# Choice of experts moved from VectorE to GpSimd, and a narrower wait at the seam between projections and attention

## The chip, the cores and the metric

One core of one Trainium2 chip runs the whole program in one launch. The metric is device time in microseconds. TensorE is PE in the tables (PEld is its weight load), VectorE is DVE, ScalarE is ACT, GpSimd is POOL, and SyncE is SP, which here only issues transfers.

## The reference, cut to what matters

The input `x` has 8 batches of 1024 tokens of 256 numbers. Two branches start from the normalised `xn`:

```
xn = layernorm(x)
s  = attention(layernorm(xn) * scale + bias) + xn      # 16 heads of 64, low-rank q/k/v, rotary, softmax
logits = xn @ router_w.T                               # 8 experts
k_probs, k_idx = top_k(softmax(logits), 2)             # normalised over the two
rank = position of this (token, choice) among all that chose the same expert
keep = rank < capacity
out_buf = silu(xn @ w1[e]) @ w2[e]                     # for each expert's kept rows
combined = sum over the two of k_probs * out_buf[e, rank] * keep
out = x + s * silu(combined + xn)
```

"The choice of experts" in this document is the arithmetic behind the two largest logits: each choice's rank in its expert's list, the row of a table in which its token is entered (`fill`), its factor in the sum (`mix`), and for each group of 256 table rows the expert whose weights it takes (`widx`).

## The kernel before, in words

The program has four stages, one behind the other on each engine: projections (`project_parts`, eight batches of 1024 tokens), attention (`attend_parts`, 64 pairs of heads), experts (`expert_parts`, 71 groups of rows), and the combination. Every engine has its own instruction list, written out by hand; there is no planner. Engines wait for each other on semaphores, and each works its list strictly in order. What changes is the seam between projections and attention, and the first pair of heads.

Projections end with the last batch's compressed vectors `cpt`. SP stores them to memory (L203) and ACT holds the wait `stored` before its first copy of attention (L1178, `pj["stored"](e)` in the prologue of `scalar`). Tiles are laid over each other: `at_rawq` and `at_rawk`, into which ACT copies the first projected queries and keys (L1130), lie over the tile from which the rows `xn` are stored; `rt_tot` and its neighbours lie over the tile from which `cpt` is stored. `stored` waits for both kinds of store.

The prologue of attention then prepares the first pair. ACT copies queries and keys out of PSUM (L1130); SP makes copies with neighbouring rows exchanged (L828, `at_swpq`, `at_swpk`); DVE turns them (L942 by the cosines, L946 the exchanged rows by the sines, L950 the sum) and makes `at_kdif` and `at_step` (L959, L966, L967); PE meanwhile computes the last batch's value vectors (L540), which ACT copies out and SP stores (L207). A loop of six steps k = 0..5 finds row maxima of the first pair: PE L1299 and L1302, then ACT L1147 (`gain`) and DVE L974 (`maximum`), for two heads in turn. In it ACT also writes and sends the negated maxima (`negate` L1162, `max_rows` L1168, two transfers that ACT itself issues), and behind it PE and ACT project and copy the third pair's queries (L1338, L1130).

`body` is one pair: eight steps g = 0..7, in each of which PE has two score tiles (L1279), two tiles of maxima, and the value products of the step before (L1292); ACT has two exponentials (L1124), two `gain`s, and copies; DVE has two maxima, running sums of the exponentials (L985) and the turning of the pair after the next. From the second pair on PE also has two sets of denominators (L1346), which ACT copies out (`den_copy` L1157). The next pair's first maxima come out of this pair's steps, so that an engine that is late by more than a step stops the others.

The choice of experts (`route_parts`) is woven into this. PE makes two products of the one-hot tiles, column totals (L621) and prefix sums (L624), into `at_st`. DVE does the rest in slices of a generator, `next(choice)`: copy of the totals (L642), running sum (L644), small sizes (L652 to L657), ranks (L661, L664) in the prologue; four products (L668, L669), four sums over the experts (L673, L675), rows (L678 to L683), factors (L686 to L690) and `widx` (L692 to L695) in the body of the first pair. PE waits with `ranked` for the ranks before its first body, ACT and POOL with `done` for everything: ACT at step g = 5 of the first pair, before `out_copy` writes `mid_osb`, which lies over the one-hot tiles and `rt_rank`; `mid_den`, first written at step g = 0 of the second pair, lies over `rt_tmp`. POOL then enters tokens in the table, pair by pair (L911 to L916). The table is first read before the last pair.

Of the kernel before, what the change touches and what calls it, by code (L numbers as in the profile page):

```python
# [99 lines left out]
def project_parts(nc, ctx, io, scr, keep):  # L100


    with ExitStack() as tiles:
# [127 lines left out]
        def stored(e):  # L231
            for s in s_xs:
                e.wait_ge(s, 16 * (NBATCH // 2 + 1))
            for s in s_cs:
                e.wait_ge(s, 32 * (NBATCH // 2 + 1))
# [267 lines left out]
        def tensor(e):  # L503
# [73 lines left out]
            with e.Fori(0, NBATCH // 2 - 1) as it:  # L577
# [6 lines left out]
                "stored": stored, "values_stored": values_stored, "chosen": chosen, "emptied": emptied}  # L584


def route_parts(nc, ctx, keep, pj):

    with ExitStack() as tiles:
# [13 lines left out]
        tmp = [by_expert(sb(f"tmp{k}", [P, C])[:, :]) for k in range(4)]  # L603
        tot, cum = sb("tot", [P, NE, NT]), sb("cum", [P, NE, NT])
        dif, p2, den = (sb(n, [P, NT]) for n in ("dif", "p2", "den"))
        rk, pos, over, kept, row, blk_of = (sb(n, [P, NT, 2])[:, :, :] for n in ("rk", "pos", "over", "kept", "row", "blk_of"))
        need, end, base = (sb(n, [P, NE]) for n in ("need", "end", "base"))
        past, who = sb("past", [P, GROUPS, NE - 1]), sb("who", [P, GROUPS])
        s_v, s_mm, s_dif, s_exp, s_mul, s_done = (sem(n) for n in ("v", "mm", "dif", "exp", "mul", "done"))
        sides = [slice(n * C // 2, (n + 1) * C // 2) for n in range(2)]  # L610

        def scalar(e):
            e.wait_ge(s_dif, 1)
            e.activation(p2[:, :], dif[:, :], ACT.Exp).then_inc(s_exp, 1)

# [11 lines left out]
        def vector(e, pt, pp):  # L627
# [12 lines left out]
            e.wait_ge(s_mm, 2)  # L640
            pj["stored"](e)
            then(e.tensor_copy(tot[:, :, :], pt.rearrange("p (t e) -> p e t", e=NE)))  # L642
            yield
            then(e.tensor_tensor_scan(flat(cum), newe[:, :], flat(tot), 0.0, ALU.mult, ALU.add))  # L644
# [6 lines left out]
            yield  # L651
            e.tensor_tensor(out=dif[:, :], in0=m[1][:, :], in1=m[0][:, :], op=ALU.subtract).then_inc(s_dif, 1)  # L652
# [3 lines left out]
            then(e.tensor_tensor_scan(end[:, :], ones[:, 0:NE], need[:, :], 0.0, ALU.mult, ALU.add))  # L656
# [3 lines left out]
            yield  # L660
            then(e.tensor_tensor(out=cum[:, :, :], in0=cum[:, :, :], in1=tot[:, :, :], op=ALU.subtract))  # L661
            yield
            e.wait_ge(s_mm, 4)
            then(e.tensor_tensor(out=rank, in0=by_expert(pp), in1=cum[:, :, :].rearrange("p e t -> p t e"), op=ALU.add))  # L664
            e.sem_inc(s_done, 1)
            for k in range(2):
                yield
                e.tensor_tensor(out=tmp[k], in0=oh[k], in1=rank, op=ALU.mult).then_inc(s_mul, 1)  # L668
                e.tensor_tensor(out=tmp[2 + k], in0=oh[k], in1=base3, op=ALU.mult).then_inc(s_mul, 1)  # L669
            for k in range(2):  # L670
                yield
                e.wait_ge(s_mul, 2 * k + 1)
                e.tensor_reduce(out=rk[:, :, k], in_=tmp[k], axis=AX.X, op=ALU.add).then_inc(s_mul, 1)  # L673
                e.wait_ge(s_mul, 2 * k + 2)
                e.tensor_reduce(out=pos[:, :, k], in_=tmp[2 + k], axis=AX.X, op=ALU.add).then_inc(s_mul, 1)  # L675
            yield
            e.wait_ge(s_mul, 8)
# [3 lines left out]
            then(e.scalar_tensor_tensor(out=row, in0=row, scalar=float(NSLOT // P), in1=blk_of, op0=ALU.mult, op1=ALU.add))  # L681
            then(e.tensor_scalar(over, rk, float(CAP), FAR, ALU.is_ge, ALU.mult))
            e.tensor_tensor(out=keep["fill"][:, :, :], in0=row, in1=over, op=ALU.add).then_inc(s_done, 1)  # L683
            yield
# [6 lines left out]
            yield  # L691
            then(e.tensor_tensor(out=past[:, :, :], in0=grp[:, :].unsqueeze(2).broadcast_to((P, GROUPS, NE - 1)),  # L692
                                 in1=end[:, 0:NE - 1].unsqueeze(1).broadcast_to((P, GROUPS, NE - 1)), op=ALU.is_ge))
            then(e.tensor_reduce(out=who[:, :], in_=past[:, :, :], axis=AX.X, op=ALU.add))
            e.tensor_scalar(keep["widx"][:, :], who[:, :], float(P), part[:, 0:1], ALU.mult, ALU.add).then_inc(s_done, 1)  # L695

        def ranked(e):
            e.wait_ge(s_done, 1)
# [4 lines left out]
        return {"vector": vector, "scalar": scalar, "tensor": tensor, "ranked": ranked, "done": done}  # L703


def attend_parts(nc, ctx, below, bridge, io, scr, keep, pj, rt):


    with ExitStack() as tiles:
# [195 lines left out]
        def gpsimd(e):  # L905
            def body(i, *_):
                if isinstance(i.n(), int) and i.n() == 0:
                    pj["blanked"](e)
                    rt["done"](e)
# [9 lines left out]
            def prologue():  # L919
                e.memset(zeros[:, :], 0.0).then_inc(s_blank, 1)  # L920
                e.wait_ge(s_blank, 1)

# [10 lines left out]
        def vector(e, ex_vector):  # L933
# [74 lines left out]
            choice = rt["vector"](e, *route_at)  # L1008

            def prologue():  # L1010
# [16 lines left out]
                for k in range(6):  # L1027
# [6 lines left out]
                    if k in (3, 5):  # L1034
                        next(choice)
# [7 lines left out]
                    if k >= 3:  # L1043
                        next(choice)
# [4 lines left out]
            def body(i, prev, ahead):  # L1049
# [3 lines left out]
                for g in range(NG):  # L1053
# [38 lines left out]
                    if not prev and g < 4:  # L1092
                        next(choice, None)
                        next(choice, None)
                    if not prev and g == 4:
                        for _ in choice:
                            pass
                        e.memset(ones[:, :], 1.0)
# [19 lines left out]
        def scalar(e, pj_value, ex_scalar):  # L1118
# [52 lines left out]
            def prologue():  # L1171
# [6 lines left out]
                pj["stored"](e)  # L1178
# [12 lines left out]
                for k in range(6):  # L1191
# [1002 lines left out]
```

## Time and profile before

| | us |
|---|---|
| runs of the kernel before, median of 3 | 3825.41 (3824.31 to 3827.25) |
| profiled execution, its own time | 3827.14 |
| its span from first to last instruction | 3825.6 |
| PE busy | 3727.7 (97%) |
| DVE busy | 3382.1 (88%) |
| ACT busy | 2811.3 (73%) |
| POOL busy | 861.9 (23%) |

Busy shares are averages over the four stages. Times in the rows below count from the first instruction of the profiled execution; projections end at about 210 us, and the first pair's body begins on PE at 264.04 us.

### The profile page before, as it was taken

What the parts mean: (1) busy time and instruction counts of PE and PEld (TensorE: products, weight loads), DVE (VectorE), ACT (ScalarE), POOL (GpSimd) and SP (SyncE); (2) the same over time, 40 slices, a digit from 0 to 9 for tenths busy, and PEclk for the clock granted to TensorE, in tenths of its full rate; (3) what the DMA queues carried; (4) which work ended last, traced back from release to release, by engine and by line L of the source; (5) the groups of instructions that cost most, each with busy time, mean ns of one, the idle gap of its engine ahead of it and who ended that gap; (6) DMA issues with size and microseconds to landing.
All of it is one profiled execution on the core that took longest, in us unless ns stands there. A gap on an engine that the chain in (4) does not pass through costs nothing. (4 is left out here: it accounts for less than half of the span.)

```text
span 3825.6 us, 77720 instructions
## 1 busy us (share of the span) xinstructions
PE 3727.7 (97%) x24340; PEld 2379.8 (62%) x24340; DVE 3382.1 (88%) x4656; ACT 2811.3 (73%) x4075; POOL 861.9 (23%) x796
## 2 busy tenths in 40 slices
PE   7969999999999999999999999999999999999999
PEld 5744444444444444444444444444499999999899
DVE  8869999999999999999999999999777777777699
ACT  5757887878787878787787878787766666666565
POOL 2205544510000000000000000000166666666400
PEclk9989999999999999999999999999999999999999
DMA  7964554544444444434444444443366666666697
GB/s 262 355 226 148 153 166 150 169 134 137 126 137 126 136 126 126 136 112 140 118 139 121 137 126 137 126 134 105 115 217 218 219 217 219 220 217 220 203 367 261
DMA packets 397301, 659.74 MB, mean 172 GB/s; under 512 B 140142, under 2 KB 288751, under 8 KB 361137
## 3 DMA queue, kind: packets, MB, share of 16 engines
q1 hardware_dynamic: 349984, 449.85, 37.8%
q0 software_dynamic: 45200, 208.52, 15.8%
q8 instruction: 35, 0.57, 0.1%
q10 hardware_dynamic: 2048, 0.53, 0.1%
q14 instruction: 34, 0.27, 0.0%
HBM read 453.07 MB, written 138.81 MB: 155 GB/s over the span
## 5 line engine op out<-in xcount | busy, mean ns | idle before, releaser
L1124 ACT ACTIVATE at_ex<-at_st 128x1024 f32<-128x1024 f32 x1024 | 1047.1, 1023 | 121.8 <-PE at_st L1279 98.8
L1292 PE MATMUL at_pv<-at_ex,at_v 128*64 128x512 f32 x4096 | 992.6, 605 | 0.0
L1147 ACT ACTIVATE at_fr<-at_fr 128x512 f32<-128x512 f32 x1024 | 599.9, 586 | 343.7 <-PE at_fr L1302 291.0
L974 DVE TENSOR_REDUCE at_mx<-at_fr 128x1 f32<-128x512 f32 x1024 | 703.7, 687 | 126.1 <-PE at_fr L1299 73.1
L985 DVE TENSOR_TENSOR at_sum<-at_sum,at_ex 128x1024 f32<-128x1024 f32 x512 | 624.9, 1221 | 12.7 <-ACT at_ex L1124 1.8
L1572 POOL DMA_INDIRECT seam_stage<-in_w,keep_widx x142 | 139.2, 980 | 1960.4 <-DVE at_rotk L950 1886.9
L1292 PEld LDWEIGHTS at_pv<-at_ex,at_v 128*64 128x64 f32 x4096 | 248.7, 136 | 509.6 <-issue 494.2
L1302 PE MATMUL at_fr<-at_kfar,at_qh 64*128 64x512 f32 x1024 | 466.4, 455 | 19.0 <-DVE at_mx L974 11.0
L1299 PE MATMUL at_fr<-at_kdif,at_qh 64*128 64x512 f32 x1024 | 471.5, 460 | 4.6 <-DVE at_mx L974 2.4
L1299 PEld LDWEIGHTS at_fr<-at_kdif,at_qh 64*128 64x128 f32 x1024 | 188.2, 184 | 418.9 <-issue 411.5
L1756 PE MATMUL ex_h<-ex_xT,ex_w 128*128 128x256 f32 x3408 | 423.4, 284 | 4.2 <-issue 4.2
L1772 PE MATMUL ex_o<-ex_w,ex_hT 128*128 128x256 f32 x3408 | 425.2, 284 | 0.9 <-DVE ex_out L1653 0.9
L1756 PEld LDWEIGHTS ex_h<-ex_xT,ex_w 128*128 128x128 f32 x3408 | 416.7, 193 | 6.0 <-issue 6.0
L1772 PEld LDWEIGHTS ex_o<-ex_w,ex_hT 128*128 128x128 f32 x3408 | 412.4, 191 | 1.1 <-DVE ex_out L1653 1.1
L1279 PE MATMUL at_st<-at_qh,at_kh 64*128 64x512 f32 x2048 | 405.8, 392 | 3.3 <-DMA at_top<-at_mneg 3.1
L1279 PE MATMUL at_st<-at_ql,at_kh 64*128 64x512 f32 x2048 | 403.8, 389 | 0.0
L1279 PE MATMUL at_st<-at_qh,at_kl 64*128 64x512 f32 x2048 | 403.5, 389 | 0.0
L1692 ACT ACTIVATE ex_w<-seam_stage 128x1024 fp32r<-128x1024 f32 x142 | 142.6, 1051 | 286.5 <-PE ex_o L1772 282.3
L985 DVE TENSOR_TENSOR at_sum<-at_ex 128x1024 f32<-128x1024 f32 x256 | 311.2, 1216 | 2.8 <-ACT at_ex L1124 2.8
L1578 POOL DMA_INDIRECT scr_eo<-ex_out,mid_slots x142 | 253.3, 1784 | 221.8 <-DVE ex_out L1653 168.2
L1302 PEld LDWEIGHTS at_fr<-at_kfar,at_qh 64*128 64x128 f32 x1024 | 188.2, 184 | 93.6 <-issue 76.3
L1279 PEld LDWEIGHTS at_st<-at_qh,at_kl 64*128 64x128 f32 x2048 | 193.7, 184 | 44.6
(183 smaller groups left out, 5657.1 us busy)
## 6 DMA issues: line engine op xcount, KB each, us to landing
at_cq<-scr_c SPq DMA_DIRECT2D x62, 1024.0 KB
at_ck<-scr_c SPq DMA_DIRECT2D x62, 1024.0 KB
scr_v<-pj_v SPq DMA_DIRECT2D x64, 512.0 KB, 6.7
at_swpq<-at_rawq SPq DMA_DIRECT2D x128, 256.0 KB
at_swpk<-at_rawk SPq DMA_DIRECT2D x128, 256.0 KB
at_v<-scr_v SPq DMA_DIRECT2D x64, 512.0 KB
mid_rec<-scr_rec SPq DMA_DIRECT2D x256, 128.0 KB
scr_o<-mid_oT SPq DMA_DIRECT2D x64, 512.0 KB
```

Source lines behind the costliest of these rows:

```text
L974: e.reduce_max(mx[k // QB][:, h * QB + k % QB:h * QB + k % QB + 1], fr[h][:, :], AX.X).then_inc(s_tr[h], 1)
L985: e.tensor_tensor(out=acc, in0=ex[k - 1][:, :, :] if first else acc, in1=ex[k][:, :, :], op=ALU.add).then_inc(s_sum, 1)
L1124: e.activation(ex[k][:, :, :], st[u % 2][:, :, :], ACT.Exp, scale=SCALE).then_inc(s_exp, 1)
L1147: e.activation(fr[h][:, :], fr[h][:, :], ACT.Relu).then_inc(s_pos[h], 1)
L1279: mm = e.matmul(st[u % 2][:, h, :], kk[rows[h], :] if t == 3 else kk[rows[h], keys], qq[rows[h], bank[n]], start=(t == 0 and kt < 2), stop ...
L1292: mm = e.matmul(pv[n][rows[h], :], v[i.u][:, kt, rows[h]], ex[kt][:, h, :], start=(kt == 0), stop=(kt == KT - 1))
L1299: return e.matmul(fr[h][:, :], query_tile(j, k, h), kdif[j.u][rows[h], :], start=True, stop=True)
L1302: return e.matmul(fr[h][:, :], query_tile(j, k, h), kfar[j.u][rows[h], :], start=False, stop=True, skip_group_check=True)
L1578: e.indirect_dma_start(out=scr["eo"], out_offset=bass.IndirectOffsetOnAxis(ap=slots[:, g * GT + c:g * GT + c + 1], axis=0), in_=out[g % 2] ...
L1692: e.activation(w2_half(a.u, 0, k), half2(raw2[a.u], k), ACT.Copy).then_inc(s_w2h, 1)
L1756: mm = e.matmul(phid[:, j, f % 2 * GP:(f % 2 + 1) * GP], w1[q][:, ws, f, k, :], xT[q][:, xs, k, :], start=(ws + xs + k == 0), stop=(ws == ...
L1772: mm = e.matmul(po[:, c, 0:D], hT[q][:, hh, f, c * P:(c + 1) * P], w2[q][:, ws, f, :], start=(hh + ws + f == 0), stop=(hh == 1 and f == NF ...
```

## The change

There are four edits.

1. ACT's first wait of attention becomes `rows_stored`, which waits for the stores of the rows `xn` only. The wait for the stores of `cpt` stays in front of the copy of the totals.
2. ACT takes both products out of PSUM (`take_total` at k = 2, `take_prefix` at k = 3). DVE keeps one instruction of the choice, the running sum over 512 columns, now at k = 5.
3. Everything else of the choice is written again for POOL, as one list of 50 instructions behind the sum, each waiting for the one before. Sums over the experts become three additions of halves, a scan of eight becomes a copy and seven additions, the reciprocal becomes a power of -1, the comparison of groups with ends becomes seven compares and four additions, and a fused operation becomes two.
4. PE waits for the two copies instead of the ranks; DVE (g = 4) and ACT (g = 5) of the first pair wait for POOL's products (`spread`); ACT waits for all of the choice (`done`) at g = 0 of the second pair; ACT's exponential of the choice moves from g = 1 to g = 2. At the end of the prologue ACT sends the negated maxima behind `gain(first, 4, 1)` and not ahead of it, and the first half of the third pair's queries is projected at k = 4 and copied at k = 5.

```diff
+        def rows_stored(e):
+            for s in s_xs:
+                e.wait_ge(s, 16 * (NBATCH // 2 + 1))
         def stored(e):
-            for s in s_xs:
-                e.wait_ge(s, 16 * (NBATCH // 2 + 1))
+            rows_stored(e)
...
+        def vector(e):
+            e.wait_ge(s_taken, 1)
+            e.tensor_tensor_scan(cum[...], newe[:, :], tot[...], 0.0, ALU.mult, ALU.add).then_inc(s_scan, 1)
+        def take_total(e, pt):
+            e.wait_ge(s_mm, 2)
+            pj["stored"](e)
+            e.activation(tot[:, :, :], pt.rearrange("p (t e) -> p e t", e=NE), ACT.Copy).then_inc(s_taken, 1)
+        def take_prefix(e, pp):
+            e.wait_ge(s_mm, 4)
+            e.activation(rank, by_expert(pp), ACT.Copy).then_inc(s_taken, 1)
...
+        def gpsimd(e):
+            e.wait_ge(s_taken, 1)
+            e.tensor_tensor(out=dif[:, :], in0=m[1][:, :], in1=m[0][:, :], op=ALU.subtract).then_inc(s_dif, 1)
+            e.wait_ge(s_scan, 1)
...
-            then(e.tensor_tensor_scan(end[:, :], ones[:, 0:NE], need[:, :], 0.0, ALU.mult, ALU.add))
+            then(e.tensor_copy(end[:, 0:1], need[:, 0:1]))
+            for k in range(1, NE):
+                then(e.tensor_tensor(out=end[:, k:k + 1], in0=end[:, k - 1:k], in1=need[:, k:k + 1], op=ALU.add))
...
+            for k in range(2):
+                then(e.tensor_tensor(out=by_expert(tmp[:, k, :]), in0=oh[k], in1=rank, op=ALU.mult))
+                then(e.tensor_tensor(out=by_expert(tmp[:, 2 + k, :]), in0=oh[k], in1=base3, op=ALU.mult))
             e.sem_inc(s_done, 1)
-            for k in range(2):
-                e.tensor_reduce(out=rk[:, :, k], in_=tmp[k], axis=AX.X, op=ALU.add).then_inc(s_mul, 1)
-                e.tensor_reduce(out=pos[:, :, k], in_=tmp[2 + k], axis=AX.X, op=ALU.add).then_inc(s_mul, 1)
+            for n in (NE // 2, NE // 4, NE // 8):
+                then(e.tensor_tensor(out=each[:, :, 0:n], in0=each[:, :, 0:n], in1=each[:, :, n:2 * n], op=ALU.add))
...
-            then(e.reciprocal(keep["mix"][:, :, 0], den[:, :]))
+            then(e.tensor_scalar(dif[:, :], ones[:, 0:NT], -1.0, None, ALU.mult))
+            then(e.tensor_tensor(out=keep["mix"][:, :, 0], in0=den[:, :], in1=dif[:, :], op=ALU.pow))
...
-            then(e.tensor_tensor(out=past[:, :, :], in0=grp..., in1=end..., op=ALU.is_ge))
-            then(e.tensor_reduce(out=who[:, :], in_=past[:, :, :], axis=AX.X, op=ALU.add))
+            for k in range(NE - 1):
+                then(e.tensor_scalar(past[:, :, k], grp[:, :], end[:, k:k + 1], None, ALU.is_ge))
+            then(e.tensor_tensor(out=past[:, :, 0:3], in0=past[:, :, 0:3], in1=past[:, :, 3:6], op=ALU.add))
+            then(e.tensor_tensor(out=past[:, :, 0:1], in0=past[:, :, 0:1], in1=past[:, :, 6:7], op=ALU.add))
+            then(e.tensor_tensor(out=past[:, :, 0:1], in0=past[:, :, 0:1], in1=past[:, :, 1:2], op=ALU.add))
+            then(e.tensor_tensor(out=who[:, :], in0=past[:, :, 0], in1=past[:, :, 2], op=ALU.add))
+            then(e.tensor_scalar(who[:, :], who[:, :], float(P), part[:, 0:1], ALU.mult, ALU.add))
+            e.tensor_copy(keep["widx"][:, :], who[:, :]).then_inc(s_done, 1)
...
         def ranked(e):
+            e.wait_ge(s_taken, 2)
+        def spread(e):
             e.wait_ge(s_done, 1)
...
@@ attention, ACT
-                pj["stored"](e)
+                pj["rows_stored"](e)
...
+                    if k == 2:
+                        rt["take_total"](e, route_at[0])
+                    if k == 3:
+                        rt["take_prefix"](e, route_at[1])
                     if k == 4:
                         negate(first, 0)
-                        e.wait_ge(s_init, 2)
-                        max_rows(first, 0)
+                    if k == 5:
+                        proj_copy(third, Q, 0, pv[1])
                     gain(first, k, 1, s_y)
+                    if k == 4:
+                        e.wait_ge(s_init, 2)
+                        max_rows(first, 0)
-                for n in range(NH2):
-                    proj_copy(third, Q, n, pv[1])
+                proj_copy(third, Q, 1, pv[1])
...
                     if g == 5 and not prev:
+                        rt["spread"](e)
+                    if g == 0 and isinstance(i.n(), int) and i.n() == 1:
                         rt["done"](e)
@@ attention, PE
-                e.wait_ge(s_raw[K], 4)
-                project(third, Q, 0, pv[1])
+                    if k == 4:
+                        e.wait_ge(s_raw[K], 4)
+                        project(third, Q, 0, pv[1])
```

## Rows read from the trace of the kernel before

**Rows 1.** The page: busy time of the engines, their shares of the span.
```profile
PE 3727.7 (97%) x24340; PEld 2379.8 (62%) x24340; DVE 3382.1 (88%) x4656; ACT 2811.3 (73%) x4075; POOL 861.9 (23%) x796
```

**Rows 2.** Timeline of ACT at the seam: start, length, line, [idle before].
```profile
207.43 1.03 ACT L445 ACTIVATE pj_c<-pj_pa 128x1024 f32<-128x1024 f32 x1 [0.86 <-PE pj_pa L554]
224.39 1.09 ACT L1130 ACTIVATE at_rawq<-at_pv 128x512 f32<-128x512 f32 x2 [15.94 <-DMA scr_c<-pj_cpt]
```

**Rows 3.** Timeline of SP's queue at the seam.
```profile
207.91 2.94 SPq L203 DMA_DIRECT2D scr_c<-pj_cpt  x2
225.50 1.19 SPq L828 DMA_DIRECT2D at_swpq<-at_rawq  x2
```

**Rows 4.** Windows: us, busy PE, PEld, DVE, ACT, POOL; PEclk, DMA share, GB/s.
```profile
211.00:214.00 3.00, 0.00 (x0) 0.00 (x0) 0.00 (x0) 0.00 (x0) 0.00 (x0) 0.71 1.04 419
...
220.00:223.00 3.00, 0.00 (x0) 0.00 (x0) 0.00 (x0) 0.00 (x0) 0.00 (x0) 0.50 0.84 352
...
229.00:232.00 3.00, 3.00 (x14) 2.42 (x13) 2.97 (x3) 1.48 (x2) 0.00 (x0) 0.94 0.53 210
...
264.04:301.94 37.90, 30.20 (x161) 15.45 (x162) 35.42 (x55) 23.88 (x35) 6.62 (x10) 0.92 0.38 119
```

**Rows 5.** Timeline of DVE, prologue and first body.
```profile
228.52 1.22 DVE L946 TENSOR_TENSOR at_swpq<-at_swpq,at_sin 128x1024 f32<-128x1024 f32 x1 [1.10 <-DMA at_swpq<-at_rawq]
...
260.85 1.03 DVE L664 TENSOR_TENSOR rt_rank<-at_st,rt_cum 128x512 f32<-128x512 f32 x1
...
265.83 0.68 DVE L974 TENSOR_REDUCE at_mx<-at_fr 128x1 f32<-128x512 f32 x1
```

**Rows 6.** Timeline of PE, from the prologue to the second body.
```profile
238.18 0.50 PE L1299 MATMUL at_fr<-at_kdif,at_qh 64*128 64x512 f32 x1
...
267.54 0.38 PE L1299 MATMUL at_fr<-at_kdif,at_qh 64*128 64x512 f32 x1
...
310.53 0.50 PE L1299 MATMUL at_fr<-at_kdif,at_qh 64*128 64x512 f32 x1
...
312.71 0.39 PE L1299 MATMUL at_fr<-at_kdif,at_qh 64*128 64x512 f32 x1
```

**Rows 7.** Timeline of ACT at the end of the prologue; ACTq is its transfers' issue.
```profile
255.02 1.81 ACTq L1168 DMA_DIRECT2D at_top<-at_mneg  x2
256.87 0.58 ACT L1147 ACTIVATE at_fr<-at_fr 128x512 f32<-128x512 f32 x1 [1.94 <-issue]
```

**Rows 8.** Waits in 262 to 311 us: total, times, longest.
```profile
PE at_fr L1302 <- DVE at_mx L974: 6.9, 4, 3.6
```

**Rows 9.** Timeline of PE: denominators in the middle of the second and third body.
```profile
332.53 1.07 PE L1346 MATMUL at_pv<-at_sum,mid_ones 128*32 128x512 f32 x8
372.14 1.07 PE L1346 MATMUL at_pv<-at_sum,mid_ones 128*32 128x512 f32 x8
```

**Rows 10.** Timeline of POOL, small and powering instructions and a fill.
```profile
1.04 0.21 POOL L269 MEMSET early_zero<- 128x142 int32 x1
...
16.24 0.29 POOL L275 TENSOR_SCALAR pj_veps<-pj_mv 128x4 f32<-128x4 f32 x1 [1.70 <-DVE pj_mv L331]
16.61 1.05 POOL L277 TENSOR_TENSOR pj_rstd<-pj_veps,pj_minus_half 128x4 f32<-128x4 f32 x1
...
184.95 2.21 POOL L259 TENSOR_TENSOR pj_rstd<-pj_veps,pj_minus_half 128x8 f32<-128x8 f32 x1 [0.18 <-POOL pj_veps L257]
187.12 0.52 POOL L920 MEMSET at_zeros<- 128x512 f32 x1
...
318.71 1.25 POOL L911 COPY at_fill_i<-keep_fill 128x2 int32 x1 [4.03 <-DMA scr_table<-at_tok_i,at_fill_i]
```

**Rows 11.** Line L259: ns min/median/max of one, first and last start.
```profile
L259 POOL TENSOR_TENSOR pj_rstd<-pj_veps,pj_minus_half x14: 1665/1686/2570, 24.5 to 185.0; 128x8 f32<-128x8 f32 x14
```

**Rows 12.** Timeline of DVE beside POOL's instruction at 184.95.
```profile
185.67 1.23 DVE L395 TENSOR_TENSOR pj_cpt<-pj_c,pj_cpt 128x1024 fp32r<-128x1024 f32 x1
```

**Rows 13.** POOL's groups by line: busy us, mean ns of one, idle before.
```profile
L911 POOL COPY at_fill_i<-keep_fill 128x2 int32 x56 | 34.8, 621 | 182.1 <-DMA scr_table<-at_tok_i,at_fill_i 182.1
L912 POOL COPY at_tok_i<-keep_tok 128x2 int32 x56 | 15.0, 269 | 0.0
```

More of the change, by code:

```diff
@@ L602, in route_parts @@
         oh = [by_expert(early[f"oh{k}"][:, :]) for k in range(2)]
-        tmp = [by_expert(sb(f"tmp{k}", [P, C])[:, :]) for k in range(4)]
+        tmp = sb("tmp", [P, 4, C])
         tot, cum = sb("tot", [P, NE, NT]), sb("cum", [P, NE, NT])
         dif, p2, den = (sb(n, [P, NT]) for n in ("dif", "p2", "den"))
-        rk, pos, over, kept, row, blk_of = (sb(n, [P, NT, 2])[:, :, :] for n in ("rk", "pos", "over", "kept", "row", "blk_of"))
+        over, kept, row, blk_of = (sb(n, [P, NT, 2])[:, :, :] for n in ("over", "kept", "row", "blk_of"))
         need, end, base = (sb(n, [P, NE]) for n in ("need", "end", "base"))
         past, who = sb("past", [P, GROUPS, NE - 1]), sb("who", [P, GROUPS])
-        s_v, s_mm, s_dif, s_exp, s_mul, s_done = (sem(n) for n in ("v", "mm", "dif", "exp", "mul", "done"))
+        s_v, s_mm, s_dif, s_exp, s_taken, s_scan, s_done = (sem(n) for n in ("v", "mm", "dif", "exp", "taken", "scan", "done"))
         sides = [slice(n * C // 2, (n + 1) * C // 2) for n in range(2)]
@@ L670, in vector @@
-            for k in range(2):
-                yield
-                e.wait_ge(s_mul, 2 * k + 1)
-                e.tensor_reduce(out=rk[:, :, k], in_=tmp[k], axis=AX.X, op=ALU.add).then_inc(s_mul, 1)
-                e.wait_ge(s_mul, 2 * k + 2)
-                e.tensor_reduce(out=pos[:, :, k], in_=tmp[2 + k], axis=AX.X, op=ALU.add).then_inc(s_mul, 1)
-            yield
-            e.wait_ge(s_mul, 8)
+            e.wait_ge(s_taken, 2)
+            then(e.tensor_tensor(out=rank, in0=rank, in1=cum[:, :, :].rearrange("p e t -> p t e"), op=ALU.add))
@@ L678, in vector @@
+            sums = each[:, :, 0].rearrange("p (k t) -> p t k", k=4)
+            rk, pos = sums[:, :, 0:2], sums[:, :, 2:4]
             then(e.tensor_tensor(out=row, in0=rk, in1=pos, op=ALU.add))
@@ L680, in vector @@
             then(e.tensor_scalar(blk_of, blk_of, -WHOLE, float(1 - NSLOT), ALU.add, ALU.mult))
-            then(e.scalar_tensor_tensor(out=row, in0=row, scalar=float(NSLOT // P), in1=blk_of, op0=ALU.mult, op1=ALU.add))
+            then(e.tensor_scalar(row, row, float(NSLOT // P), None, ALU.mult))
+            then(e.tensor_tensor(out=row, in0=row, in1=blk_of, op=ALU.add))
             then(e.tensor_scalar(over, rk, float(CAP), FAR, ALU.is_ge, ALU.mult))
-            e.tensor_tensor(out=keep["fill"][:, :, :], in0=row, in1=over, op=ALU.add).then_inc(s_done, 1)
-            yield
+            then(e.tensor_tensor(out=row, in0=row, in1=over, op=ALU.add))
+            e.tensor_copy(keep["fill"][:, :, :], row).then_inc(s_done, 1)
             e.wait_ge(s_exp, 1)
@@ L687, in vector @@
             then(e.tensor_scalar(den[:, :], p2[:, :], 1.0, None, ALU.add))
[L688 removed]
+            then(e.tensor_scalar(dif[:, :], ones[:, 0:NT], -1.0, None, ALU.mult))
+            then(e.tensor_tensor(out=keep["mix"][:, :, 0], in0=den[:, :], in1=dif[:, :], op=ALU.pow))
             then(e.tensor_tensor(out=keep["mix"][:, :, 1], in0=p2[:, :], in1=keep["mix"][:, :, 0], op=ALU.mult))
             e.tensor_tensor(out=keep["mix"][:, :, 0:2], in0=keep["mix"][:, :, 0:2], in1=kept, op=ALU.mult)
[L691 to L695 removed]
+            for k in range(NE - 1):
[6 more added lines that the diff above has]
+            e.tensor_copy(keep["widx"][:, :], who[:, :]).then_inc(s_done, 1)
         def ranked(e):
+            e.wait_ge(s_taken, 2)
+        def spread(e):
             e.wait_ge(s_done, 1)
@@ L701, in done @@
             e.wait_ge(s_done, 3)
-        return {"vector": vector, "scalar": scalar, "tensor": tensor, "ranked": ranked, "done": done}
+        return {"gpsimd": gpsimd, "vector": vector, "scalar": scalar, "take_total": take_total, "take_prefix": take_prefix, "tensor": tensor, "ranked": ranked, "spread": spread, "done": done}
 def attend_parts(nc, ctx, below, bridge, io, scr, keep, pj, rt):
@@ L921, in prologue @@
                 e.wait_ge(s_blank, 1)
+                pj["blanked"](e)
+                rt["gpsimd"](e)
+                rt["done"](e)
             def tail(i):
@@ L1033, in prologue @@
                         turn_sin(second, Q)
-                    if k in (3, 5):
-                        next(choice)
                     if k == 4:
@@ L1042, in prologue @@
                         turn_add(second, Q)
-                    if k >= 3:
-                        next(choice)
+                    if k == 5:
+                        rt["vector"](e)
                 turn_cos(second, K)
```

34 lines of the change are left out of this document (7 added, 27 removed).

## The prediction, made blind

> **What bounds the kernel now.** I read the page's busy times first: PE is busy for 97% of the span, DVE 88%, POOL 23% [rows 1], so time can be won only where PE stands. The timeline of ACT shows the longest such place: it ends the projections' last copy at 208.46 and starts attention's first at 224.39, after 15.94 us of waiting for the store of `cpt` [rows 2]. The windows say what goes on meanwhile: no engine works, the transfer engines are full at 419 GB/s until about 222.5, and PE's clock falls from 2.4 to 1.2 GHz, to be back at 0.94 of full in 229 to 232 [rows 4]. The second place is the first body. Its window has 30.2 us of PE in 37.9 [rows 4], and the waits of that stretch put 6.9 us on DVE's maxima being late, once 3.6 us, which is where DVE does slices of the choice [rows 8]. From the middle of the second body to that of the third takes 372.14 - 332.53 = 39.6 us [rows 9]; the first took 310.53 - 264.04 = 46.5, the latter being the start of its window [rows 4, 6].
>
> **1, the narrower wait.** ACT can start at 208.5: 15.9 us sooner. I don't count that. SP issues the last two stores of `cpt` from 207.91 [rows 3] and would issue the exchanged rows right behind, at about 211, when the transfer engines have work until 222.5. If a queue is served in order, those rows (two times 256 KB, 1.2 us at 419 GB/s) arrive at 222.5 + 1.2 + 1.8 = 225.5, with 1.8 us from last byte to release as at the store (222.5 to 224.3). DVE started on them at 228.52 [rows 5], so it is 3.0 us sooner, and from there its chain is as long as before. The exchanged keys stand behind them and a value tile (another 2.4 us, 228), in time for DVE, which has 3.6 us of work before them. PE idles from about 214.5 to 229.6 instead of 210 to 225, so it restarts at 1.2 GHz as before; I work out ACT's order with that (turned queries 228.0, second queries 229.1, PE's second keys 229.6 and value tile to 235.1) and get the loop's first L1299 at 235.1 where it was 238.18 [rows 6]. **Term: -3.1 us.** Bounds: 0 if arrival slips by three more, -14 if the rows overtook the backlog.
>
> **2, the prologue's loop.** DVE loses the totals' copy, the sizes and the ranks. ACT gains two copies of 512 columns, 0.6 us each, at k = 2 and 3, where it has about 1.1 us idle between gains: nothing. The gain behind the transfers' issue idled 1.94 us [rows 7]; with the issue moved behind it, the issue delays the next gain instead, so 0.8 us remains. The scan (1.2 us) takes the place of the ranks (1.03 us, start 260.85 [rows 5]): it starts at 260.85 - 0.8 - 3.1 = 256.9 and **ends at 258.1**. The turning of keys behind it ends at 261.6, the maximum that was at 265.83 [rows 5] is done at 262.2, and PE's second L1299 of the body, 267.54 before [rows 6], can go then: 5.3 us sooner.
>
> **3, the first body without DVE's slices.** PE's own work in a body is 39.6 us, less two sets of denominators (2.0) and the value products that the first body doesn't have (1.9): 35.7. Of it 2.5 lie ahead of that L1299, so the second body could start at 262.2 + 33.2 + 1 (slow clock at the head) + 3 (DVE, below) = 299.4, **11 us sooner** than 310.53 [rows 6].
>
> **4, POOL's list, and the new wait.** ACT holds `done` at the head of the second body, with all its gains and exponentials behind it, and PE after two score tiles has nothing. So the question is when POOL is done. Its list starts at 258.1. Each of 50 instructions waits for the one before: from start to start of two small ones it is 16.61 - 16.24 = 0.37 us [rows 10]; I take 0.36.
> - 34 instructions up to the power: 12.2 us fixed. Six over 512 columns and three over 1024, 512 and 256 make 4864 elements with two inputs. No row has such a one on POOL. From below, a fill takes (0.52 - 0.21) / 370 = 0.84 ns a column [rows 10], 4.1 us in all; from above, the power's 153 ns a column (next item) can't be meant for an addition, so I take three fills' worth (two inputs, one output), 2.5 ns: 12.2 us. The smaller ones, 64 to 128 columns, 2.6 us. Together 27.0.
> - The power over 64 columns: 1.05 us for 4 columns [rows 10], 1.686 for 8 [rows 11], so 0.157 a column (0.153 by medians) and 64 make 10.3 us, with its handover 10.4.
> - 15 instructions behind it: 5.4 fixed, 2.6 in elements: 8.0.
> - Beside DVE. A copy of two columns took 1.25 us at 318.71 where DVE ran a two-input instruction [rows 10], and clean ones take 0.18; over 56 pairs the means are 0.621 and 0.269 [rows 13], 0.28 us above clean. On 34 instructions 9.5 us. Once ACT stands, DVE soon does too, so nothing for the last 15. Bounds: 0, and 1.04 for each.
>
> Sum: 258.1 + 27.0 + 9.5 + 10.4 + 8.0 = **313.0**. ACT is ready at 299.4. It stalls for some 13 us; the second body's second L1299, 312.71 before [rows 6], goes 0.7 us after `done`, at 313.7: +1.0. After so long a pause the clock is at 1.2 GHz for some 4 us, as at 225 to 229 [rows 4], which costs 2.1. **Sum against the profiled execution: +3.1 us**; all that edits 1 to 3 win is spent in that wait. The profiled execution took 3827.14, 1.7 above the median of the runs, so 3828.5.
>
> The other new waits: the products are due at 258.1 + 22 = 280; DVE asks at g = 4, some 8 us later, ACT at g = 5. POOL's table entries start 20 us later; they ended at about 800 and are needed near 2700. PE's `ranked` now waits for ACT's copies, long made. What POOL does costs DVE something, the 3 us above: 24 of DVE's 36 us are instructions with two inputs in SBUF.
>
> The Trainium skill speaks against this change: "SBUF — State Buffer", on the shared port pair, says that GpSimd and a VectorE instruction with two SBUF inputs exclude each other for a whole instruction, and whoever starts first holds the ports. The trace agrees for POOL as the one that waits [rows 10, 13]. The other way it doesn't show it: a powering instruction runs from 184.95 to 187.16 and DVE's two-input one inside it takes its usual 1.23 us [rows 12]. By the same skill's "GPSIMD Engine Reference", § 3.1, an addition of 2048 columns takes 4497 ns, 2.2 a column; with that the sum would be 1.5 us less.
>
> **Rivals.**
> *A, POOL is later, the kernel slower.* One mechanism: POOL loses a race for each instruction. If each of the 34 costs 1.04 more, 62 us of them stand before the power instead of 27 + 9.5. Up to 301, when DVE stops, 43 are done; the rest goes clean, 8.3 us: 309.3, and `done` at 309.3 + 18.4 = 327.7. The end moves by 15.7 + 2.1 = +17.8: 3843. It decides from `done` at 317.5 on, where the loss passes 0.2%. For it: a chain of 50 dependent steps has 50 chances; against it: DVE's maxima, 11 us of the body, have one input out of PSUM.
> *B, POOL is early, the gain stays.* With the fill's rate for elements and no loss beside DVE: 258.1 + 17.4 + 10.4 + 6.2 = 292, ahead of ACT. Then the end moves by -11: 3814. For it: nothing but the lower bounds. It decides below `done` at 304.
> *C, POOL holds DVE.* By the skill's rule above: POOL's long instructions (12 us, 63% of them against a DVE that wants two inputs) and the power's 10 us keep DVE back by 18 us, less its slack of 4. The second body then starts at 309, and the end is 3824 to 3826 even if POOL is done by 304. Its sign is that the two-input DVE instructions of the first body grow or stand behind gaps.
> *D, the exchanged rows overtake the stores.* Everything up to the scan comes up to 8 us sooner, POOL too: `done` at 305, the end at -7 to -5: 3819 to 3821.
>
> **How the numbers follow.** Forecast (`done` between 304 and 317.5) 0.35, A 0.32, B 0.16, C 0.1, D 0.07. Below 0.2%, 7.65 us either way, this kernel's change can't be told from none. Faster: B and a part of D, 0.2; same: the forecast, C, the rest of D, 0.48; slower: A, 0.32. The range takes A to near its end and B nearly whole: 3815 to 3842.
>
> **What would show it.** Right: ACT's first copy near 208.5, L946 near 225.5, the loop's first L1299 near 235, and at the second body ACT idle for about 13 us with POOL as what ends it, POOL's last copy near 313, one powering instruction of 10 us. If ACT has no such wait, step 4 is wrong and the kernel is faster by about 11 us. If L946 starts by 216, step 1 is wrong. If DVE asks at g = 4 before the products are there, a second stall of DVE shows in the middle of the first body.

## The result, and the profile after

The changed kernel takes 3830.91 us (median of 20 runs, 3828.08 to 3833.72), the one before 3825.61 (20 runs, 3823.40 to 3829.26): a ratio of 1.0014, with a 95% interval of 1.0009 to 1.0020. The forecast was 3828.5, which is 2.4 us too low and on the right side of zero. The prediction held that less than 0.2% can't be told from none; with 20 runs of each, 0.14% can: the kernel is slower by some 5 us (3.4 to 7.7).

The profiled execution took 3828.08 us (span 3826.5, mean clock 0.992), 0.94 more than the profiled one of before. It is the lowest of its 20 runs, 2.8 below their median, where before's was 1.5 above: that is how 0.94 in the traces and 5.3 in the medians belong together. So I read order and mechanism from the traces, and price from medians.

The page of after, busy time by engine. Against [rows 1], POOL has 58 us and 51 instructions more, DVE 33 instructions and 6 us less, PE the same:
```profile
PE 3726.2 (97%) x24340; PEld 2378.7 (62%) x24340; DVE 3376.4 (88%) x4623; ACT 2813.2 (74%) x4077; POOL 920.0 (24%) x847
```
The 33 instructions that DVE no longer has took 14.0 us in before, but its busy time falls by only 5.7: the first sign that what is left runs longer.

The seam in after: timelines of ACT, SP's queue and DVE (start, length, line, [idle before]), answering to [rows 2, 3, 5]:
```profile
206.40 1.08 ACT L1138 ACTIVATE at_rawq<-at_pv 128x512 f32<-128x512 f32 x2
...
205.97 2.95 SPq L203 DMA_DIRECT2D scr_c<-pj_cpt  x2
209.14 2.15 SPq L844 DMA_DIRECT2D at_swpq<-at_rawq  x2
...
223.49 1.23 DVE L962 TENSOR_TENSOR at_swpq<-at_swpq,at_sin 128x1024 f32<-128x1024 f32 x1 [13.25 <-DMA at_swpq<-at_rawq]
```
And its windows, in the columns of [rows 4]:
```profile
211.00:214.00 3.00, 3.00 (x15) 2.50 (x14) 0.00 (x0) 1.95 (x2) 0.00 (x0) 1.00 1.03 419
220.00:223.00 3.00, 0.00 (x0) 0.00 (x0) 0.00 (x0) 0.00 (x0) 0.00 (x0) 0.56 0.99 407
```
ACT's copy starts 18 us sooner, the exchanged rows are issued 16 us sooner, and DVE gets them 5.0 us sooner. This execution reached the end of the projections 1.94 us earlier (PE's first product with `cq`: 205.20, before 207.14), so the edit brought 3.1. The idle time has not gone, it has moved: PE is busy in 211 to 214, where it was idle, and idle in 220 to 223, where it was idle too, with the transfers still at 407 GB/s.

PE from the prologue to the third body, answering to [rows 6, 9]:
```profile
231.91 0.50 PE L1315 MATMUL at_fr<-at_kdif,at_qh 64*128 64x512 f32 x1
...
254.27 0.80 PE L1315 MATMUL at_fr<-at_kdif,at_qh 64*128 64x512 f32 x1
...
258.88 0.50 PE L1315 MATMUL at_fr<-at_kdif,at_qh 64*128 64x512 f32 x1
...
299.52 0.50 PE L1315 MATMUL at_fr<-at_kdif,at_qh 64*128 64x512 f32 x1
...
312.18 0.79 PE L1315 MATMUL at_fr<-at_kdif,at_qh 64*128 64x512 f32 x1
312.90 1.93 PE L1362 MATMUL at_pv<-at_sum,mid_ones 128*32 128x512 f32 x8
314.76 2.49 PE L1308 MATMUL at_pv<-at_ex,at_v 128*64 128x512 f32 x8
...
333.83 1.06 PE L1362 MATMUL at_pv<-at_sum,mid_ones 128*32 128x512 f32 x8
...
372.81 1.06 PE L1362 MATMUL at_pv<-at_sum,mid_ones 128*32 128x512 f32 x8
```
The second body starts at 299.52, 11.0 us sooner than before. PE has two score tiles, then idles for 10.3 us, and its next L1315 comes 12.7 us behind the last. It restarts at the lower of its two clocks: the windows give a granted clock of 0.50 (1.2 GHz) in 312 to 314 us, 0.76 in 314 to 318 and 1.00 in 318 to 322, and the denominators take 1.93 us for 1.06. The next denominators come 1.3 us later than before. ACT's timeline there:
```profile
298.25 0.60 ACT L1138 ACTIVATE at_rawq<-at_pv 128x512 f32<-128x512 f32 x1
311.54 0.58 ACT L1155 ACTIVATE at_fr<-at_fr 128x512 f32<-128x512 f32 x1 [12.68 <-POOL keep_widx L708]
```
The waits of 250 to 330 us (who waits for whom, total, times, longest) name the same releaser, and PE behind ACT:
```profile
ACT at_fr L1155 <- POOL keep_widx L708: 12.7, 1, 12.7
...
PE at_fr L1318 <- ACT at_fr L1155: 10.7, 2, 10.3
...
PE at_fr L1318 <- DVE at_mx L990: 6.7, 7, 1.5
```
POOL's timeline, the list that ends that wait:
```profile
254.71 1.15 POOL L665 TENSOR_SCALAR rt_need<-rt_cum 128x8 f32<-128x8 f32 x1 [12.58 <-DVE rt_cum L621]
...
261.35 1.38 POOL L674 TENSOR_TENSOR rt_cum<-rt_cum,rt_tot 128x512 f32<-128x512 f32 x1
262.81 2.13 POOL L676 TENSOR_TENSOR rt_rank<-rt_rank,rt_cum 128x512 f32<-128x512 f32 x1
265.02 2.16 POOL L678 TENSOR_TENSOR rt_tmp<-early_oh,rt_rank 128x512 f32<-128x512 f32 x1
...
292.83 10.64 POOL L698 TENSOR_TENSOR keep_mix<-rt_den,rt_dif 128x64 f32<-128x64 f32 x1
303.55 0.35 POOL L699 TENSOR_TENSOR keep_mix<-rt_p,keep_mix 128x64 f32<-128x64 f32 x1
...
304.42 4.30 POOL L702 TENSOR_SCALAR rt_past<-early_grp,rt_end 128x71 f32<-128x71 f32 x7
...
311.27 0.24 POOL L708 CAST keep_widx<-rt_who 128x71 int32<-128x71 f32 x1
```
`done` comes at 311.51. Behind the second and third body nothing differs: in the window 345 to 2700 us PE is busy for 2345.76 us (before 2346.07), and from PE's fifth group of denominators (392.29, before 391.64) to the end of the span it is 3434.2 us (3434.0).

### The profile page after: what moved, and what is told of

The parts are those of the page before. It is cut to its first block and busy times, and to the rows that moved or that the text cites. A ratio compares the mean times of both kernels' runs of the same rounds, so it can differ in the third digit from the quotient of the medians.

```text
span 3826.5 us, 77737 instructions
## 1 busy us (share of the span) xinstructions
PE 3726.2 (97%) x24340; PEld 2378.7 (62%) x24340; DVE 3376.4 (88%) x4623; ACT 2813.2 (74%) x4077; POOL 920.0 (24%) x847
## 5 line engine op out<-in xcount | busy, mean ns | idle before, releaser
L1318 PE MATMUL at_fr<-at_kfar,at_qh 64*128 64x512 f32 x1024 | 467.4, 456 | 29.0 <-DVE at_mx L990 10.7
L1315 PE MATMUL at_fr<-at_kdif,at_qh 64*128 64x512 f32 x1024 | 472.5, 461 | 2.3 <-DVE at_mx L990 2.3
L1315 PEld LDWEIGHTS at_fr<-at_kdif,at_qh 64*128 64x128 f32 x1024 | 188.6, 184 | 416.7 <-issue 406.9
```

The source lines that it names most:

```text
L1315: return e.matmul(fr[h][:, :], query_tile(j, k, h), kdif[j.u][rows[h], :], start=True, stop=True)
L1318: return e.matmul(fr[h][:, :], query_tile(j, k, h), kfar[j.u][rows[h], :], start=False, stop=True, skip_group_check=True)
```

## The experiments

Each was timed beside the kernel before on one chip; the ratio is to it, with its 95% interval. To compare seams in traces without the projections' own scatter (first product with `cq` between 204.6 and 207.5), I also take the distance from that product to PE's fifth group of denominators: 184.50 us before (to 391.64), 187.09 after (to 392.29). A difference between the medians of two of these kernels is uncertain by about 2 us either way, by 3 where one has only 5 runs (an estimate, by drawing again from the runs of each).

**e1: the wide wait back.** In the changed kernel ACT waits for `cpt` as before.
```
-                pj["rows_stored"](e)
+                pj["stored"](e)
```


> The changed kernel with edit 1 undone: ACT again waits for the stores of cpt before attention's first copy. Theory (the end follows the moment at which POOL has finished its list, and that list starts with the scan): the scan and all of POOL's list come 3 us later, ACT's wait at the second body stays 12 to 13 us long, and the time is 3 us over the changed kernel, about 3834. Rival (narrower wait is worth nothing, since the exchanged rows arrive behind the stores in any case): L946's counterpart starts no later than in the changed kernel, and the time stays at 3831.

Measured 3832.86, ratio 1.0023 (1.0014 to 1.0032): 2.0 above the changed kernel. Its timelines of ACT and DVE:
```profile
223.03 1.08 ACT L1138 ACTIVATE at_rawq<-at_pv 128x512 f32<-128x512 f32 x2 [15.90 <-DMA scr_c<-pj_cpt]
...
227.15 1.23 DVE L962 TENSOR_TENSOR at_swpq<-at_swpq,at_sin 128x1024 f32<-128x1024 f32 x1 [1.08 <-DMA at_swpq<-at_rawq]
```
The wait is back to its 15.9 us, DVE starts 3.0 us later once the ends of the projections are set equal (227.15 - 205.82 = 21.33 against 18.29), and 2.0 us reach the end by medians (2.6 with each held against its own runs of before). A wait of 15.9 us was worth 2 to 3 us, give or take 2. ACT's stall at the second body stayed as long, 12.72 us: the list of POOL starts as much later as the bodies do, so the stall hides nothing of this.

**e5: the seam alone.** The kernel before with the narrower wait and the moved operations, the choice still on DVE.
```
 (before)
-                pj["stored"](e)
+                pj["rows_stored"](e)
...
+                    if k == 5:
+                        proj_copy(third, Q, 0, pv[1])
                     gain(first, k, 1, s_y)
...
+                    if k == 4:
+                        e.wait_ge(s_init, 2)
+                        max_rows(first, 0)
-                for n in range(NH2):
-                    proj_copy(third, Q, n, pv[1])
+                proj_copy(third, Q, 1, pv[1])
...
```


> The kernel before with edit 1 and the moved operations of edit 4 (negated maxima sent behind the gain, third pair's queries projected at k = 4), the choice of experts left on DVE. Theory: the exchanged rows arrive 3 us sooner and the gain behind the transfers' issue is free 0.8 us sooner, and nothing takes it back: 3.5 to 4 us faster than the kernel before, about 3821. Rival (the moves cost something of their own, or DVE's slices of the choice swallow it): 0 against the kernel before. It also shows whether the value of edit 1 is the same without POOL's list.

Measured 3820.64 (before 3825.24), ratio 0.9986 (0.9977 to 0.9995). The seam's edits gain 4.6 us; the choice on POOL then costs 3830.91 - 3820.64 = 10 us. The whole change is a gain and a larger loss. How much of the 4.6 is the narrower wait (e1: 2 to 3) and how much the moved operations is open; no run has the latter alone. In its first body PE still waits for DVE's maxima as in [rows 8]; its waits of 262 to 311 us:
```profile
PE at_fr L1307 <- DVE at_mx L977: 6.9, 4, 3.6
```

**e6: the exchanged rows of the first pair from ACT's queue.** In the changed kernel, ACT issues them behind its copies, instead of SP.
```
-                swap_rows(At(0, 0), Q)
-                swap_rows(At(0, 0), K)
...
+                def exchange(x):
+                    e.wait_ge(s_raw[x], 2)
+                    for o in range(2):
+                        e.dma_start(swp[x][o:P:2, :], raw[x][1 - o:P:2, :]).then_inc(s_swp[x], 16)
                 copies(first, Q)
+                exchange(Q)
...
                 copies(first, K)
+                exchange(K)
```


> The changed kernel with the exchanged rows of the first pair issued by ACT, behind its copies, instead of by SP, so that they are in another queue than the stores of cpt. Theory (the 13 us for which DVE waits for them are the backlog of one queue, served in order): they arrive by 214, the prologue and POOL's list start 8 to 9 us sooner, ACT's wait at the second body stays as long, and the time falls by 8 to 9 us, to about 3822. Rival (the transfer engines are simply full until 222): they arrive at 221 or later whatever the queue, and the time stays within 1 us of 3831.

Measured 3823.45, ratio 0.9994 (0.9985 to 1.0003), 7.5 below the changed kernel. Counted from the first product with `cq` (207.06 here), the scan at 248.68 comes 6.6 us sooner than in after, and so do the second body and the fifth denominators; ACT's stall for POOL is 12.69 us as ever.

**e9: the same, with the wait released (e4, below).**


> e4 with the exchanged rows of the first pair issued by ACT. Theory (one queue served in order, and the two gains are in different places): e4's 3818 less 8 to 9, about 3809. Rival (transfer engines full): 3818.

Measured 3808.78, ratio 0.9959 (0.9945 to 0.9972): 9.1 below e4. Its timelines of ACT's queue and DVE:
```profile
207.10 1.73 ACTq L1193 DMA_DIRECT2D at_swpq<-at_rawq  x2
...
214.92 1.23 DVE L963 TENSOR_TENSOR at_swpq<-at_swpq,at_sin 128x1024 f32<-128x1024 f32 x1 [5.08 <-DMA at_swpq<-at_rawq]
```
And windows of it:
```profile
208.00:212.00 4.00, 4.00 (x19) 3.31 (x18) 1.69 (x5) 2.00 (x3) 0.00 (x0) 1.00 1.03 417
...
222.00:227.00 5.00, 4.64 (x16) 2.71 (x15) 2.06 (x4) 4.59 (x7) 0.00 (x0) 0.86 1.01 414
```
The transfer engines are as full as ever (417 and 414 GB/s), and DVE gets the rows 8.6 us sooner than in after, 8.2 counted from the first product with `cq` (204.79). Some 1.6 us of it is that ACT issues them sooner than SP, which is still issuing stores; the rest is their place behind SP's stores in one queue. The engines' rate wasn't what held them. In 222 to 227 us PE is busy for 4.64 of 5 us, where after has it idle. The Trainium skill, "DMA: Bandwidth & Descriptors", "Queues, rings and completion order", says that each transfer engine goes round the queues that have work, a packet at a time; by that, a second queue gets its share at once, and the trace agrees.

**e2: the scan earlier.** DVE's scan at k = 3 of the prologue's loop instead of k = 5.
```
-                    if k == 5:
+                    if k == 3:
                         rt["vector"](e)
```


> The changed kernel with DVE's scan at k = 3 instead of k = 5, which gives POOL its start about 8 us sooner. Theory: POOL's last instruction ends at about 304 instead of 311.5, ACT's wait shrinks from 12.7 to about 5 us, and the time falls by 7 to 8 us, to about 3823. Rival (the gain was eaten by DVE, which POOL's long instructions hold): DVE's long instructions are as long as before, ACT's wait is not what sets the end, and the time moves by less than 2 us.

Measured 3822.83 (3822.30 without one execution of 5080.85), ratio 0.9994 (0.9984 to 1.0003): 8.1 to 8.6 below the changed kernel. The scan comes at 246.62, `done` at 305.2, and ACT's stall shrinks from 12.7 to 7.6, by its timeline:
```profile
305.24 0.58 ACT L1155 ACTIVATE at_fr<-at_fr 128x512 f32<-128x512 f32 x1 [7.55 <-POOL keep_widx L708]
```
By medians 8 of the 13 us that the stall turns out to be worth (e4) thus hang on when the list starts. The traces show less: the stall shrinks by 5.1, and the distance to the fifth denominators by 4.8 (see the end of this section).

**e3: no power.** A product in its place, so the factors that weigh the experts are not computed.
```
-            then(e.tensor_tensor(out=keep["mix"][:, :, 0], in0=den[:, :], in1=dif[:, :], op=ALU.pow))
+            then(e.tensor_tensor(out=keep["mix"][:, :, 0], in0=den[:, :], in1=dif[:, :], op=ALU.mult))
```


> The changed kernel with the power replaced by a product of the same tiles (the factors in the sum are then not the reference's): POOL's list is 10.3 us shorter and nothing else changes. Theory: ACT's wait falls from 12.7 to about 2.5 us and, with less of a pause for the clock, the time falls by 10 to 12 us, to 3819 to 3821. Rival (DVE held by POOL): the power barely touches DVE in the trace, so the time would stay within 2 us of 3831.

Measured 3825.26, ratio 1.0000 (0.9991 to 1.0009): 5.6 less than the changed kernel, where I had put 10 to 12. Its timelines of POOL and ACT:
```profile
292.45 0.33 POOL L698 TENSOR_TENSOR keep_mix<-rt_den,rt_dif 128x64 f32<-128x64 f32 x1
...
295.49 7.69 POOL L702 TENSOR_SCALAR rt_past<-early_grp,rt_end 128x71 f32<-128x71 f32 x7
...
306.00 0.58 ACT L1155 ACTIVATE at_fr<-at_fr 128x512 f32<-128x512 f32 x1 [7.53 <-POOL keep_widx L708]
```
The list lost 10.3 us of power and became only 5.1 shorter (51.7 us from its first instruction to `done`, after 56.8). The seven comparisons behind it take 7.69 us instead of 4.30, and the two products ahead of them 1.21 and 1.36 instead of 0.35 and 0.46, since they now run while DVE still works; in after the comparisons ran in the silence that the stall itself had made. The other runs bear that out: the comparisons take 4.29 us in e6, which has the whole stall, and 7.30 to 8.62 in e4, e7, e8 and e9, which have none. My expectation priced them at what they cost in that silence.

**e4: ACT released earlier.** ACT's wait at the second body is for POOL's sums instead of the whole list (`kept` moves ahead of that mark), and DVE waits for the whole at g = 6, ahead of the first pair's normalisation.
```
+            then(e.tensor_scalar(kept, rk, float(CAP), None, ALU.is_lt))
             e.tensor_copy(keep["fill"][:, :, :], row).then_inc(s_done, 1)
...
+        def summed(e):
+            e.wait_ge(s_done, 2)
...
                     if g == 0 and isinstance(i.n(), int) and i.n() == 1:
-                        rt["done"](e)
+                        rt["summed"](e)
...
+                    if g == 6 and isinstance(i.n(), int) and i.n() == 1:
+                        rt["done"](e)
```


> The changed kernel with ACT's wait at the second body cut down to what its copy overwrites: kept is computed before fill is handed on, ACT waits for the second mark (fill) instead of the third, and DVE waits for the third at g = 6 of the second body before its first normalised output. Theory: POOL's second mark comes at about 292, before ACT asks at 299, so the wait is gone, and with it 12.7 us less about 1 of slack plus about 1.5 of clock: 3817 to 3819, faster than the kernel before by 7 to 8. Rival (POOL's long instructions delay the first body anyway and the pause is not what costs): less than 3 us. Second rival: the wait moves to DVE at g = 6 (about 325), which is later than POOL's last mark at 311, so it should not show.

Measured 3817.85, ratio 0.9981 (0.9972 to 0.9990): 13.1 below the changed kernel, for the same work. ACT has no wait for POOL any more, though POOL ends later than in after. Its timelines of POOL and PE:
```profile
318.20 1.08 POOL L708 CAST keep_widx<-rt_who 128x71 int32<-128x71 f32 x1
...
302.35 1.06 PE L1367 MATMUL at_pv<-at_sum,mid_ones 128*32 128x512 f32 x8
...
322.08 1.06 PE L1367 MATMUL at_pv<-at_sum,mid_ones 128*32 128x512 f32 x8
```
The last copy itself takes 1.08 us instead of 0.24, beside a DVE that is at work. The denominators keep 1.06 us, and the granted clock is 1.00 in 302 to 306 us: no pause, no fall of the clock. This is the experiment that shows the cause: the stall was worth 13 us (12.4 with each held against its own runs of before, 10.8 by the distances in the traces).

**e7: e4 with e2's early scan.**


> The previous kernel e4 (ACT's wait cut down to what its copy overwrites) with DVE's scan at k = 3. Theory: without a wait at the second body the start of POOL's list no longer sets anything; what is left is POOL's long instructions holding DVE, now partly in the prologue, where DVE has idle time: equal to e4 within 2 us, 3816 to 3819. Rival (the end still follows POOL's list): another 7 us less, 3811.

Measured 3814.62, ratio 0.9973 (0.9962 to 0.9985). 3.2 below e4, and 2.4 by the distances in the traces; neither is clear of the 2 us that I had allowed. With no stall left an early list helps a little, probably since more of it runs in the prologue, where DVE has gaps.

**e10: e7 with each of POOL's four products over 512 columns issued twice.**
```
-                then(e.tensor_tensor(out=by_expert(tmp[:, k, :]), in0=oh[k], in1=rank, op=ALU.mult))
-                then(e.tensor_tensor(out=by_expert(tmp[:, 2 + k, :]), in0=oh[k], in1=base3, op=ALU.mult))
+                for _ in range(2):
+                    then(e.tensor_tensor(out=by_expert(tmp[:, k, :]), in0=oh[k], in1=rank, op=ALU.mult))
+                    then(e.tensor_tensor(out=by_expert(tmp[:, 2 + k, :]), in0=oh[k], in1=base3, op=ALU.mult))
```


> e7 (ACT's wait cut down, scan at k = 3) with each of POOL's four products over 512 columns issued twice; the second gives the same values again. POOL's second mark moves from 279 to about 288, still ahead of ACT at 297, so no wait of ACT can carry the effect. Theory (POOL's two-input instructions hold DVE's): each added one holds a DVE instruction for about 1 us, DVE sets the pace of the first body, and the time rises by 3 to 4 us over e7, to about 3818. Rival (POOL only waits for DVE, as the copies of the kernel before did): DVE's instructions keep 1.22 us and the time stays within 1 us of 3814.6.

Measured 3817.39 (before 3825.89), ratio 0.9978 (0.9968 to 0.9988). That is 2.8 us above e7, by itself hardly more than the medians can tell. The traces carry it: in e10 the second body starts 2.4 us later than in e7 (95.5 us behind the first product with `cq`, e7 93.2), the fifth denominators come 2.4 later too, and PE's waits for DVE's maxima in the first body (L1323, in e10 L1324) grow from 3.9 to 6.3 us, while neither ACT nor DVE has a wait for POOL in either. Four more products on an engine for which nobody waits cost 2.4 to 2.8 us, 0.6 to 0.7 each.

**e8: e4, e2 and e6 together.**


> ACT's wait cut down, scan at k = 3 and the exchanged rows of the first pair issued by ACT, all three. Theory (each takes time at another place: e9 gained 9 us over e4, e7 3 us over e4): 3808.8 less 2 to 3, so 3805 to 3807. Rival (the start of POOL's long instructions in the prologue's loop, which the queue has now made denser with value tiles, costs what it gains): 3809 again.

Measured 3808.16, ratio 0.9955 (0.9942 to 0.9969), the fastest of all by median, 0.6 below e9 (0.9959), where I had put 2 to 3. Five runs of each can't tell 0.6 from either zero or 2; the traces have 1.4. It lies between my theory and its rival, and doesn't decide.

The two measures side by side, each against the kernel before in us, by the distance to the fifth denominators in the profiled execution and by the median against the runs of before beside it:

| | trace | medians |
|---|---|---|
| after | +2.6 | +5.3 |
| e1 | +7.9 | +7.9 |
| e2 | -2.3 | -2.7 |
| e3 | -1.6 | +0.3 |
| e4 | -8.2 | -7.1 |
| e5 | -4.8 | -4.6 |
| e6 | -4.0 | -1.8 |
| e7 | -10.5 | -10.6 |
| e8 | -17.6 | -17.7 |
| e9 | -16.1 | -16.5 |
| e10 | -8.2 | -8.5 |

In seven of the eleven they agree within 0.5. After is 2.7 short in its trace, and e3 and e6 some 2, so a difference read from one of these traces alone can be off by as much.

## Why the prediction was right

**Step 1** (-3.1 us) held in time and in reason: the exchanged rows wait out the backlog of their own queue. L962 came 3.1 us sooner by the projections' end, the loop's first L1315 4.3 sooner, 1.2 more than I had worked out. The 1.2 is the execution's and not the edit's: in e2, e4, e5 and e10, which have the same seam, that L1315 comes 3.0 to 3.3 us sooner than before, in after, e3 and e7 4.1 to 4.3. By medians e1 puts the step at 2.0. e5 has it with the moved operations at 4.6. My other bound, -14 if the rows overtook, was not idle: e6 and e9 found another 7.5 and 9.1 us with a second queue, on top of this step.

**Step 2** put the scan's end at 258.1 and PE's second L1299 at 262.2; with this execution's 1.94 us added back they were 256.6 and 260.8. The extra 1.2 us of step 1 are in both.

**Step 3** put the second body's start at 299.4; it was 299.52, or 301.5 with the 1.94. So a stretch that began 1.4 early ended 2.1 late: the body lost 3.5 us more than my 3 for DVE. From the body's second L1315 to the second body it took 40.64 us (before 42.99, and I had 37.2): of the 5.8 us that I had expected there, 2.35 came. PE still waits 6.7 us for DVE's maxima (the waits above, all of it in the prologue's end and the first body), as in [rows 8], though DVE's slices have gone. DVE's timeline of the first body shows where:
```profile
261.51 2.03 DVE L983 TENSOR_TENSOR at_step<-at_rotk 128x768 f32<-128x768 f32 x1
...
264.07 1.95 DVE L1001 TENSOR_TENSOR at_sum<-at_ex 128x1024 f32<-128x1024 f32 x1
265.94 2.32 DVE L971 TENSOR_TENSOR at_ql<-at_rotq,at_qh 128x1024 fp32r<-128x1024 f32 x1
...
274.57 2.78 DVE L958 TENSOR_TENSOR at_rotq<-at_rawq,at_cos 128x1024 f32<-128x1024 f32 x1
...
296.08 1.22 DVE L962 TENSOR_TENSOR at_swpk<-at_swpk,at_sin 128x1024 f32<-128x1024 f32 x1
```
Instructions of 1.22 us (0.95 the first) take 1.95 to 2.78 beside POOL's long ones. Over the body I sum 7.2 us of such lengthening; my 3 and the 3.5 more make 6.5. That such lengthening reaches the end, e10 shows. This is rival C's mechanism, at less than half of its price of 18: its condition holds for two-input instructions over hundreds of columns, but not for the power. The last row above lies inside the 10.64 us of L698 and has its usual 1.22, as [rows 12] had. (C's own sum has a slip: 3 us for DVE replaced by 18 - 4 puts the second body at 310.4, not 309; its end of 3824 to 3826 holds either way.) The Trainium skill, "SBUF — State Buffer", "Who interferes with whom", has whoever comes first hold the shared pair for the whole instruction: the first four rows agree with it, the last doesn't.

**Step 4** is the one that carried the forecast. Where I put POOL's list at 54.9 us, 258.1 to 313.0, it took 56.8, 254.71 to 311.51. Up to the power 38.1 (I: 36.5), the power with its handover 10.7 (10.4), the rest 8.0 (8.0). Stall 12.68 (some 13), PE 0.7 behind `done` as said, and the restart at 1.2 GHz. Within the first part the long instructions cost 2.1 to 2.2 us beside DVE and 1.3 to 1.4 clean (I had 1.28 + 0.36 from one handover to the next, and 0.28 for the contention of any instruction). Rival A, a loss of 1.04 each, had one thing right: where a small instruction meets DVE, it does lose about 1 (L665 takes 1.15, in e2 0.27). Not all 34 meet it.

**The sum**: I had +3.1 on the profiled execution, and by medians it is +5.3. e5 and e4 split it, all against before's 3825.61: the seam -5.0 (3820.64; -4.6 beside its own runs of before), the choice on POOL with the stall taken away -2.8 (3817.85), the stall and its slow restart +13.1 (3830.91). The prediction had these as -11 in all and +14.1. The sum of mine was closer than its parts, because a gain that I had put too high (-11 for -7.8 by e4) and a stall somewhat too dear (14.1 for 13.1) cancel in part; so much of it is luck. These differences have the 2 us either way of the medians. Rival B (3814) is what e4 would have been by my terms; e4 stood at 3817.9, and what is missing is about the 3.5 us that the body lost in step 3. D did not happen: in one queue the rows did not overtake.

Open is how far a single pair of traces can be trusted here: from the projections' end to the fifth denominators they differ by 2.6 us, below the interval of the medians (3.4 to 7.7). Two places account for most of what after's trace is short. Its loop starts 1.1 to 1.3 us earlier than that of e2, e4, e5 and e10 with the same seam, and from the denominators behind the stall to the next it takes 20.9 us, where e1, e2 and e3, which have a stall too, take 21.7 to 22.1 (e6 20.9). What decides between the two lengths, no run shows.

## What to carry to other kernels

When work moves to an idle engine, price the moment at which its result is asked for, and ask for no more than the next step needs: here one wait on the whole list, where the half was wanted, turned a gain of 8 us into a loss of 5. A wait of 16 us behind a full queue was worth 2 to 3; the same rows on another queue were worth 7.5 to 9, with the transfer engines as full as before. And a long instruction timed in a lull that its own stall makes is cheaper than it will be once the stall has gone.

## What the runs showed of the hardware

- POOL and DVE hold each other up both ways, with instructions of two inputs over 512 columns and more: POOL 1.27 to 1.38 us clean and 2.12 to 2.33 beside DVE, DVE 1.22 us clean and 1.95 to 2.78 beside POOL. The power takes 0.166 us a column (10.64 for 64) and hardly holds DVE: instructions of two inputs inside it keep their 1.22 us, and the pair that began just behind it (292.88) took 2.69 for 2.54.
- What lengthens the power is how it begins. Where DVE was already in an instruction of two inputs out of SBUF, it took 11.36 to 11.45 us (e2, e7, e8, e10; in e7 DVE from 280.55, POOL from 280.81); where DVE's began behind it, 10.63 to 10.65 (after, e4, e6, e9), though in e4 and e9 DVE worked all through it.
- Seven dependent additions of one column take 2.13 us together in after and 1.80 to 1.81 in e2, e7 and e8, 0.26 to 0.30 each; I had 0.36.
